# Non-local attention block: normalising the weighted sums instead of the probability tiles

## What is computed

```python
g     = (einsum('bchw,oc->bhwo', x, w_g) + b_g).reshape(B, N, Ci)
theta = (einsum('bchw,oc->bhwo', x, w_theta) + b_theta).reshape(B, N, Ci)
phi   = (einsum('bchw,oc->bohw', x, w_phi) + b_phi[:, None, None]).reshape(B, Ci, N)
att   = softmax(einsum('bnc,bcm->bnm', theta, phi), axis=-1)
y     = einsum('bnm,bmc->bnc', att, g).reshape(B, H, W, Ci)
out   = einsum('bhwc,oc->bohw', y, w_out) + b_out[:, None, None]
inv   = bn_gamma / sqrt(bn_var + BN_EPS)
return x + out * inv[:, None, None] + (bn_beta - bn_mean * inv)[:, None, None]
```

## Time and profile before

| | us |
|---|---|
| median of 3 runs | 225.07 |
| the three runs | 225.07, 227.15, 224.91 |
| time of the profiled execution | 224.65 |
| its span in the profile | 222.8 |

### The profile page before, as it was taken

How to read it: one execution, slowest core, us unless ns; L and a number is a source line. 1 busy time by engine, 2 the same in 40 slices (tenths; PEclk the granted TensorE clock), 3 DMA queues, 4 the chain that set the end, 5 groups by cost and what they waited for, 6 DMA issues and landing times.

```text
span 222.8 us, 4289 instructions
## 1 busy us (share of the span) xinstructions
PE 214.5 (96%) x1228; PEld 141.5 (63%) x1228; DVE 183.9 (83%) x328; ACT 169.8 (76%) x311; POOL 148.6 (67%) x143
## 2 busy tenths in 40 slices
PE   7997889999999999999999999999999999999994
PEld 6684748656665767657676666647686566656552
DVE  0789998779988699779997799797997799898761
ACT  2687977869688787869698687878878696868751
POOL 2647977786787577966787687866777843843420
PEclk9999999999999999999999999999999999999999
DMA  5107330365106531185104551085200751010102
GB/s 159 72 0 200 79 100 3 108 177 141 47 4 195 135 99 49 43 236 145 47 0 140 151 133 47 0 231 153 61 27 1 188 141 47 0 47 0 50 0 94
DMA packets 8716, 19.78 MB, mean 89 GB/s; under 512 B 1536, under 2 KB 2048, under 8 KB 8704
## 3 DMA queue, kind: packets, MB, share of 16 engines
q1 hardware_dynamic: 8416, 19.50, 31.6%
q10 hardware_dynamic: 288, 0.14, 0.2%
HBM read 4.43 MB, written 4.19 MB: 39 GB/s over the span
## 4 chain that ended last, share of the span: by engine, by line
PE 85%; DVE 6%; DMA 4%; ACT 1%; POOL 1%; issue 0%; SPq 0%; ACTq 0%; DVEq 0%
PE ps_flip L663 25%; PE ps_scores L601 25%; PE ps_y L616 12%; PE ps_y L620 8%; PE ps_misc L628 6%; PE ps_misc L687 4%; PE ps_misc L702 3%; DVE neg_max L496 2%; DMA phi_ll<-lo 2%; DMA vec<-vectors_dram 2%; DVE pt_lo L566 1%; PE ps_misc L607 1%; PE ps_misc L709 1%; DVE phi_ll L484 1%; DVE g_parts L550 1%; ACT L403 1%
## 5 line engine op out<-in xcount | busy, mean ns | idle before, releaser
L316 POOL TENSOR_SCALAR probs<-probs,inv_sum 128x1024 f32<-128x1024 f32 x64 | 72.2, 1127 | 58.3 <-DVE inv_sum L518 58.2
L566 DVE SCALAR_TENSOR_TENSOR pt_lo<-ps_flip,pt_hi 128x512 f16<-128x512 f32 x128 | 82.2, 684 | 25.3 <-ACT pt_hi L446 24.3
L446 ACT ACTIVATE pt_hi<-ps_flip 128x512 f16<-128x512 f32 x128 | 69.7, 597 | 31.6 <-PE ps_flip L663 31.5
L496 DVE TENSOR_REDUCE neg_max<-ps_scores 128x1 f32<-128x1024 f32 x64 | 77.7, 1214 | 0.6 <-PE ps_scores L601 0.5
L663 PEld LDWEIGHTS ps_flip<-ident,probs 128*128 128x128 f32 x512 | 56.9, 141 | 24.7 <-issue 10.3
L455 ACT ACTIVATE probs<-ps_scores,neg_max 128x1024 f32<-128x1024 f32 x64 | 71.8, 1122 | 0.0
L663 PE MATMUL ps_flip<-ident,probs 128*128 128x128 f32 x512 | 68.4, 277 | 3.4 <-POOL probs L316 1.6
L601 PE MATMUL ps_scores<-phi_hh,theta_hl 128*128 128x512 f32 x128 | 45.5, 436 | 0.5 <-DVE phi_ll L484 0.3
L601 PE MATMUL ps_scores<-phi_ll,theta_hl 128*128 128x512 f32 x128 | 40.1, 394 | 0.0
L616 PE MATMUL ps_y<-pt_hi,g_parts 128*128 128x512 f16 (+1 forms) x128 | 32.7, 378 | 0.0
L601 PEld LDWEIGHTS ps_scores<-phi_ll,theta_hl 128*128 128x128 f32 x128 | 24.1, 188 | 5.6
(11 more groups left out here) (77 smaller groups left out, 159.6 us busy)
## 6 DMA issues: line engine op xcount, KB each, us to landing
x_in<-x_in_dram SPq DMA_DIRECT2D x16, 256.0 KB, 3.1
out_dram<-resid SPq DMA_DIRECT2D x15, 256.0 KB, 2.0
phi_hh<-hi SPq DMA_DIRECT2D x14, 256.0 KB, 4.4
phi_ll<-lo SPq DMA_DIRECT2D x14, 256.0 KB, 4.0
theta_hl<-hi SPq DMA_DIRECT2D x7, 256.0 KB, 3.4
theta_hl<-lo SPq DMA_DIRECT2D x7, 256.0 KB, 3.1
out_dram<-resid SPq DMA_DIRECT2D x1, 192.0 KB, 2.0
w_tp<-w_tp_t_dram ACTq DMA_DIRECT2D x1, 128.0 KB, 3.4
```

What stands on the lines that cost most here:

```text
L316: nc.gpsimd.tensor_scalar(out=p[:, :], in0=p[:, :], scalar1=inv_sum[:, at:at + 1], scalar2=1.0, op0=ALU.mult, op1=ALU.mult).then_inc(probs ...
L446: nc.scalar.activation(pt_hi[ring][:, c * HALF_TILES:(c + 1) * HALF_TILES, slot * P:(slot + 1) * P], ps_flip[c][:, :].rearrange("p (a n) - ...
L496: nc.vector.tensor_reduce(out=neg_max[:, k % STEPS:k % STEPS + 1], in_=ps_scores[k % 2][:, :], op=ALU.max, axis=AX.X, negate=True).then_in ...
L566: nc.vector.scalar_tensor_tensor(out=pt_lo[ring][where], in0=ps_flip[c][:, :].rearrange("p (a n) -> p a n", n=P), scalar=PROB_SCALE, in1=p ...
```

## The change

Tiles go to the transposes as they leave the exponential. 1/sum is applied to the weighted sums, where a position n is a column and not a partition, so 512 values of 1/sum are needed as a row in all 128 partitions. Two DMAs on SyncE's queue make it: `inv_to_row` writes a 128 x 4 piece of `inv_sum` as 512 single elements into a row in DRAM, and `inv_to_all` reads that row into all partitions of `inv_all`. VectorE takes one reciprocal of 128 x 4 per half. `scale_y` moves from ScalarE to VectorE and multiplies by `y_unit` and by `inv_all` in one instruction. The last half (tiles 60 to 63, `LAST_HALF`) stays as it was: a reciprocal per tile, GpSimd's scaling, and `scale_y` of its two pieces on ScalarE.

```diff
+            def inv_to_row(h):
+                if not 0 <= h < HALVES - 1:
+                    return
+                at = h * HALF_TILES % STEPS
+                sp.wait_ge(inv_sum_ready, h + 1)
+                wait(sp, inv_spread[h % 2], 16 * (h // 2))
+                sp.dma_start(inv_row[h % 2].rearrange("(t p) -> p t", p=P),
+                             inv_sum[:, at:at + HALF_TILES],
+                             allow_slow_non_contiguous=True).then_inc(inv_in_row, 16)
+            def inv_to_all(h):
+                if not 0 <= h < HALVES - 1:
+                    return
+                sp.wait_ge(inv_in_row, 16 * (h + 1))
+                wait(sp, y_scaled, h - 1)
+                sp.dma_start(inv_all[h % 2][:, :],
+                             inv_row[h % 2].unsqueeze(0).to_broadcast([P, BANK])).then_inc(inv_spread[h % 2], 16)
...
+                inv_to_row(2 * b - 1)
                 store(it, k - 2 * MT + HALF_TILES)
...
+                inv_to_all(2 * b - 1)
                 store(it, k - MT)
...
+                inv_to_row(2 * b)
+                inv_to_all(2 * b)
...
# GpSimd
-                if exists(t, TILES):
+                if in_last_half(t) and t < TILES:
...
# ScalarE
-                h = half_at(it, k - 10)
-                if j % HALF_TILES == 2 and exists(h, HALVES - 2):
-
-                    act.wait_ge(y_unit_ready, image_at(it, k - 10) + 1)
-                    scale_y(h, (k - 10) // MT % 2, ps_y[:, :], slice(0, BANK))
-                if tile_is(it, k, TILES + 1):
-                    scale_y(HALVES - 2, 1, ps_y[:, :], slice(0, BANK))
...
# VectorE
+            def scale_y(h, half, r, image, spread):
+                dve.wait_ge(y_unit_ready, image + 1)
+                dve.wait_ge(inv_spread[half], spread)
+                dve.wait_ge(y_ready, h + 1)
+                nc.vector.scalar_tensor_tensor(out=y_norm[:, :], in0=ps_y[:, :], scalar=y_unit[:, r:r + 1],
+                                               in1=inv_all[half][:, :], op0=ALU.mult,
+                                               op1=ALU.mult).then_inc(y_scaled, 1)
...
-                if exists(t, TILES):
+                if exists(t, TILES) and ((k - 1) % HALF_TILES == HALF_TILES - 1 or in_last_half(t)):
                     at = (k - 1) % STEPS
+                    cols = slice(at, at + 1) if in_last_half(t) else slice(at + 1 - HALF_TILES, at + 1)
                     dve.wait_ge(probs_ready, t + 1)
-                    nc.vector.reciprocal(inv_sum[:, at:at + 1],
-                                         row_sum[:, at:at + 1]).then_inc(inv_sum_ready, 1)
+                    nc.vector.reciprocal(inv_sum[:, cols], row_sum[:, cols]).then_inc(inv_sum_ready, 1)
+
+                h = half_at(it, k - 10)
+                if j % HALF_TILES == 2 and exists(h, HALVES - 2):
+                    scale_y(h, (k - 10) // HALF_TILES % 2, (k - 10) // MT % 2, image_at(it, k - 10),
+                            it * (8 * STEPS // HALF_TILES) + 16 * ((k - 10) // MT + 1))
+                if tile_is(it, k, TILES + 1):
+                    scale_y(HALVES - 2, 0, 1, B - 1, 8 * HALVES)
...
# TensorE, ahead of the transposes
-                    pe.wait_ge(probs_scaled, t + 1)
+                    if in_last_half(t):
+                        pe.wait_ge(probs_scaled, t - LAST_HALF + 1)
+                    else:
+                        pe.wait_ge(probs_ready, t + 1)
```

More of the change, by code:

```diff
@@ L56, in build_nonlocal_attention @@
     WARM_UP = 6
+    LAST_HALF = TILES - HALF_TILES
     LAST_PIECES = (slice(0, BANK - P), slice(BANK - P, BANK))
@@ L117, in build_nonlocal_attention @@
         y_norm = sbuf("y_norm", [P, BANK], F32)
+        inv_row = [nc.dram_tensor(f"inv_row{i}", (BANK,), F32).ap() for i in range(2)]
+        inv_all = [sbuf(f"inv_all{i}", [P, BANK], F32) for i in range(2)]
         ps_scores = [psum(f"ps_scores{i}", [P, N]) for i in range(2)]
@@ L176, in build_nonlocal_attention @@
         inv_sum_ready = sem("inv_sum_ready")
+        inv_in_row = sem("inv_in_row")
+        inv_spread = [sem(f"inv_spread{i}") for i in range(2)]
         probs_scaled = sem("probs_scaled")
@@ L204, in tile_is, with in_last_half @@
             return isinstance(it, int) and tile_at(it, k) == t
+        def in_last_half(t):
+            return isinstance(t, int) and t >= LAST_HALF
         def is_first(image):
@@ L271, in image @@
                     restack(phi_ll[1 - r], CI, lo, CI, 1 - r)
-            image(0, 0)
-            image(0, MT)
-            with sp.Fori(1, B // 2 - 1) as it:
+                inv_to_row(2 * b)
+                inv_to_all(2 * b)
+            for it in range(B // 2):
                 image(it, 0)
                 image(it, MT)
-            image(B // 2 - 1, 0)
-            image(B // 2 - 1, MT)
             store(B // 2, -2 * MT + HALF_TILES)
@@ L311, in step @@
                 t = tile_at(it, k - 1)
-                if exists(t, TILES):
+                if in_last_half(t) and t < TILES:
                     p = probs[(k - 1) % PROB_RING]
                     at = (k - 1) % STEPS
-                    hold(inv_sum_ready, t + 1)
+                    hold(inv_sum_ready, HALVES - 1 + t - LAST_HALF + 1)
                     nc.gpsimd.tensor_scalar(out=p[:, :], in0=p[:, :], scalar1=inv_sum[:, at:at + 1],
```

## The result

The change makes the kernel slower by 12%: 252.06 us (median of 4 runs, 249.88 to 253.56) against 224.99 us, ratio 1.1171 [1.1063, 1.1278]. The forecast was 224.1 us with a range up to 226.8; neither holds it.

A forecast was written before the change was run, and what follows sets the result against it. The prediction took TensorE's own work to bound the middle, leaving gains only at the ends: start -1.05, middle 0, DMAs 0, end +0.1, sum -0.95 us, so 225.07 becomes 224.1 us; range 222.9 to 226.8.

The forecast's parts named there:

- The DMAs: SyncE's queue: 15 rows and 15 spreads added; a row taken at 5 us, bounds 3.8 and 15.2, nothing lost.
- A row has 9 us there before it holds up anything at all: Odd halves on SyncE's queue: reciprocal at 136.92, restacks of `hi` issued from 145.97, so the row delays nothing.
- Idle DMA engines: Last window: DMA engines' share 0.08, given as an argument against a slow row.
- The estimate by the page: Row's landing from the skill's 2 us fixed plus 10.5 ns per packet: 7.4 us, under the 8.5 us available.
- The start: Steps 1 to 7: earlier transposes 0.57, no wait for `phi_ll` 0.20, faster first scores 0.28; gain 1.05 us.
- The middle: Full images: VectorE gets 0.88 us more work of 3.5 free; cost 0 to 0.1 per image, taken as 0.
- margin of 0.12 us: At j = 6: second bank free at 133.41, TensorE needs it at 133.53, so VectorE's scaling costs nothing.
- the end: Step 65: scaling of half 14 moves behind VectorE's `pt_lo`, ready about 214.7 against `convolve` at 214.6; +0.1 us.
- Rival A: VectorE's scaling at j = 6 takes e us over 0.65, delaying TensorE in six images; e = 0.4: 226.5 us; chance 0.19.
- Rival B: Row is slow and the end waits for it, from 8.5 us on: 226.6 to 230.8 us; chance 0.06.
- C: Nothing gained: VectorE paces the start, and the end takes back the few reciprocals; 225.0 us; chance 0.15.
- D: Start gains twice as much, TensorE's 4.5 us idle there holding more such waits; 223.0 us; chance 0.10.

The follow-up runs named there:

- rows-only kernel: Changed kernel with the 15 rows still written but no spreads, inv_all all ones, and no engine but SyncE waiting for rows: 254.83 us, ratio 1.1266.
- without DMAs: Changed kernel with neither rows nor spreads issued and inv_all filled with ones, so the factor 1/sum is left out: 223.73 us, ratio 0.9946.
- the strided read: Kernel with neither rows nor spreads and inv_all all ones, with VectorE reading inv_all at a step of four elements: 226.43 us, ratio 1.0074.

## Why the prediction was wrong

**The DMAs: the step that failed.** "A row has 9 us there before it holds up anything at all" asks only who waits for the row. It took 5 us for the landing, where the chain has 8.5 to 9.9, inside the bounds of 3.8 and 15.2. Had the size alone been wrong, the loss would have been waits for the row in the places that were named. But in the trace of the rows-only kernel nobody waits for a row, and 30.0 us are lost. The missing term is what a transfer does to those in flight beside it: `phi_ll` from at most 5.4 to as much as 14.1 us, stores from 2.0 to 6.5 in the middle, and behind them GpSimd, the restacks and TensorE. "Idle DMA engines" was read as room, and by the profile's packet times they were mostly idle during the loss too.

**The estimate by the page.** For 512 single elements it was 7.4 us by "DMA: Bandwidth & Descriptors" of the Trainium skill. The measured landing is 2.1 to 9.7 us for the same count, by address alone, so for these rows a price per descriptor is wrong in both directions (the Trainium skill has its 10.5 ns from loads issued by GpSimd, and the 2 us of fixed cost from the same path, in another section than the forecast names; these rows are stores from SyncE); the rule "rearrange so the last dim is contiguous" points the right way. The same page's section "Specifications" says that a write under 512 B is a read-modify-write. By that the elements 512 B apart would cost like those side by side, unless it matters that they share a stretch; 223.9 against 254.83 us says that something of the kind does matter.

**The start: right, a term too small.** Forecast -1.05; the peak's matmul of the first image behind it comes at 57.93 without DMAs and at 59.33 before, -1.40. The transposes of step 7 end 0.99 earlier there (29.82 against 30.81) where 0.57 was forecast. The other pieces named are seen: no wait for `phi_ll`, scores at their short time. The 0.35 left is mostly VectorE's `g_parts`, 1.31 us before and 0.96 to 0.98 in the kernels after and without DMAs. Why it was slower isn't settled: GpSimd worked beside it in the kernel before and after alike.

**The middle: right.** 0.07 per image against 0 to 0.1, and the order at j = 6 with its margin of 0.12 us is what the chain shows. It adds up to 0.4 over six images, which the forecast took as 0. The kernel without DMAs spans 222.0 us, 0.8 less than before; -1.40 + 0.4 leaves -1.0, so the end costs 0.2 (forecast 0.1). The forecast for all but the DMAs was -0.95; measured were -1.1 in the median.

**Rival A** had the right exchange rate: for e = 0.4 it said 226.5 us, and the strided read, with e = 0.40, measured 226.43. It just isn't what the change does. **Rival B** had the right cause, the row, and the wrong place: it waits at the end alone (226.6 to 230.8 us). **C and D** fall with the kernel without DMAs, -1.1 us: C had 0, and D 2.1.

## What to carry to other kernels

A small DMA is to be priced twice: for who waits for it, and for what it does to the transfers beside it; the engine time of a small DMA's own packets (72 us in all for 15 rows, beside some 30 us of loss) says nothing of the second. Single 4-byte elements should not be written side by side to DRAM while other transfers matter (29 to 38 us here); pieces of 16 B, or gaps, took the cost away, and the reordering goes to an engine with free time. Where a change brings a large unknown, one run with that part alone and nobody waiting for it says more than any reading of the waits, since here they named the store and the restack and not the culprit.

## What the runs showed of the hardware that was not expected

- 512 elements of 4 B written side by side take 9.7 us in the middle. They slow 256 KB transfers (`phi_ll`, 4.0 in the middle and 5.4 at most without them) to 5.3 and 14.1 us on the same queue, and to 13.1 and 18.0 us when they come from the other hardware queue. 64 B apart they take 2.3 us, and `phi_ll` has 4.1 and 5.5.
- The packets that get longer are those of the other transfers: 278 us of engine time more for the same 8416, against 72 us for the 7920 of the rows, 9 ns each.
- A second operand in fp32 with a step of 16 B costs VectorE 1.147 us for 512 columns instead of 0.744.
- The granted clock fell during a wait of TensorE and stayed low behind it. TensorE was busy for 4.32 of 10.2 us (windows above), and the last 4.56 were a wait for `phi_ll`; the clock was 1.00 from 116 to 117 us and 0.50, the 1.2 GHz level, from 118. It was still 0.50 in all of 119.20 to 123.00, where TensorE worked again, and 1.00, the 2.4 GHz level, from 125. Four score matmuls took 2.07 us there instead of 0.93. A wait thus costs more than its length: part of the 7.6 us by which TensorE's busy time grew.
